# Non-local attention on one core: image 0's z in three parts, image 1's phi/g split between two places, image 1's later jobs moved by half a step

## The chip, the cores and the metric

The kernel runs on one core of a Trainium2 chip. The metric is the device time of one execution in microseconds (us), as the median of several runs. The engines that matter are TensorE (PE; its weight loads are listed as PEld), VectorE (DVE), ScalarE (ACT), GpSimd (POOL) and SyncE (SP), whose queue issues most of the DMAs.

## The reference

For each of four images x of 128 channels by 1024 pixels (32 x 32), two layers follow one another:

```python
# layer 0: no softmax, so it is one matrix per image
theta, phi, g = (W_i @ x + b_i for each)            # 64 x 1024 each
pairwise = theta.T @ phi / 1024
y = pairwise @ g.T                                   # 1024 x 64
z = x + out_w @ y.T + out_b                          # 128 x 1024
# layer 1: softmax attention on z
scores = (Wt @ z + bt).T @ (Wp @ z + bp) / sqrt(128) # 1024 x 1024
out = z + Wc @ (softmax(scores, rows) @ z.T).T + bc
```

## The kernel before, in words

Layer 0 is folded into z = A x + d with a 128 x 128 matrix A per image. The jobs for it are: `pg0` and `pg1` (phi and g of the two halves of the pixels, 4 chunks of 128 each, `phi_g_chunks`, L227, copied with the bias by DVE, `copy_pg`, L639), `MT` (their product, L245), `R` (L249), `A` (L254), `Z0` and `Z1` (L264). Layer 1 is folded into t = U z + u (jobs `t0`, `t1`, L272) and scores = t.T z, and the values V = Wc z (jobs `V0` to `V2`, L286). Each job is a group of matmuls into the one PSUM bank `aux`; an engine copies it out and only then may the next job write the bank. `AUX_ORDER` (L54) lists the jobs in their order, and the waits count along it (`aux_before`, `aux_after`). Most products are made of three matmuls of a high and a low part (`three`, L220), so each result is copied twice: ACT writes the high part, DVE or POOL what is left of it.

The attention works through 32 tiles of 128 rows (`n`, 8 per image; `t` is the tile within the image). Per tile: `scores(n)` on PE (6 matmuls of 512 columns into `ring`, two tiles deep), `row_max(n)` on DVE (L680), `row_shift(n)` on POOL (L821), `exps(n)` on ACT (L523), `norm(n)` on DVE (L688), `turn(n)` on PE (8 transposes into `turned`), `high_turned` on ACT (L531), `low_turned` on DVE (L695), and a quarter of `attend` of the group of four tiles before (6 matmuls into `numer`, from n = 4 on).

Every engine runs its own list of instructions strictly in order. The lists are written out by hand as loops over n. On PE (L438) step n is: `scores(n+2)`, the next image's `early_job(t)`, `turn(n)`, `attend`, the next image's `late_job(t)`. On ACT (L611): `late_job(t-1)`, `early_job(t)`, `high_turned(n)`, `exps(n+2)`. On DVE: `late_job(t-1)`, `row_max(n+2)`, `norm(n+1)`, `early_job(t)`, `low_turned(n)`. On POOL: `row_shift(n+2)`, then splits of x, z or the first values. The jobs of image 1 run beside the tiles of image 0, when there is nothing to attend to yet for n = 0 to 3: MT early at t = 1, R late at t = 1, A early at 2, Z0 late at 2, Z1 early at 3, t0 early at 4.

Ahead of the loop stands a prologue for image 0 with banks and semaphores of its own. Its z is made in two halves into `ring` (L385), high parts at L554, low parts at L718. Its t is made in three parts (`FIRST_T`: 128, 384 and 512 columns; L559, L725). Between these PE makes pg0 of image 1 into `aux` and pg1 into `numer`. On POOL the prologue is: the parts of U, X_hi of image 1 (L788), image 0's z as a sum of its parts (L808, twice), the first half of X_lo of image 1 (L792), `row_shift(0)`, the second half of X_lo, the split of the first values (L844, L846), `row_shift(1)`.

Of the kernel before, what the change touches and what calls it, by code (L numbers as in the profile page):

```python
# [5 lines left out]
F32 = mybir.dt.float32  # L6
# [7 lines left out]
C = 128  # L14
# [34 lines left out]

Z_BUFFERS = 3  # L50
# [4 lines left out]
AUX_ORDER = ([(0, "MT"), (0, "R"), (0, "A"), (1, "pg0"), (0, "t1")] + [(1, job) for job in JOBS[2:]]  # L55
# [19 lines left out]
def build(nc, x, pg_weights, pg_bias, inner, weights, out):  # L75
    with ExitStack() as ctx:
# [61 lines left out]
        tp_ready, tp_copied = sem("tp_ready"), sem("tp_copied")  # L138
        u_ready, u_copied, u_hi, u_lo = sem("u_ready"), sem("u_copied"), sem("u_hi"), sem("u_lo")
# [34 lines left out]

        def chunks_of(bank, part):
            first, last = V_PARTS[part]
            return bank[:, 0:(last - first) * V_COLS].rearrange("p (j c) -> p j c", c=V_COLS)


        @block.sync  # L180
        def _(sp):
            for half in range(HALVES):
                sp.dma_start(X[:, 0, columns(half)], x[0, :, columns(half)]).then_inc(first_loaded[half], 16)
            sp.dma_start(w[:, :], weights[:, 0:2 * C]).then_inc(w_loaded, 16)
            sp.dma_start(VW[:, 0:C], weights[:, W_C:W_C + C]).then_inc(conv_loaded, 16)
            sp.dma_start(X[:, 1, :], x[1]).then_inc(x_loaded[1], 16)

            def load(b):
                if b == 2:
                    sp.wait_ge(first_z, HALVES)  # L190
                else:
                    sp.wait_ge(first_pg_copied, HALVES + 1)
                    sp.wait_ge(aux_free, aux_after(1, "pg0"))
# [25 lines left out]
        def _(pe):  # L219
# [7 lines left out]
            def phi_g_chunks(b, bank, half):  # L227
                for n, j in enumerate(half_range(half)):
# [67 lines left out]
            def scores(n):  # L296
                b, t = divmod(n, TILES)
                if b == 0:
                    pe.wait_ge(first_t_lo, 1 if t == 0 else 2)
                if t == GT or (b and t == 0):  # L300
                    pe.wait_ge(aux_free, aux_after(b, "t0" if t < GT else "t1"))
                if b and t == 0:
                    pe.wait_ge(z_lo, b * HALVES)
                if n >= 2:
                    pe.wait_ge(probs_ready, n - 1)
                for half in range(HALVES):
                    if n == 0:
                        pe.wait_ge(first_z_lo, half + 1)
                    mm = scores_half(n, half)
                mm.then_inc(scores_ready, 1)  # L310
# [53 lines left out]

            pe.wait_ge(pad_ready, 2)
# [6 lines left out]
            nc.tensor.transpose(turned[:, C:2 * C], w[:, W_P:W_P + C], identity[:, :]).then_inc(tp_ready, 1)  # L372
            job_A(0)
            pe.wait_ge(tp_copied, 1)
            pe.wait_ge(bias_loaded, 16)
            theta_b, phi_b = bias[:, B_T:B_T + 1], bias[:, B_P:B_P + 1]
            UT_bank = turned[:, BANK:BANK + C + 3]
            nc.tensor.matmul(UT_bank[:, 0:C], T_w, P_w, start=True, stop=True)
            nc.tensor.matmul(UT_bank[:, C:C + 1], P_w, theta_b, start=True, stop=True)
            nc.tensor.matmul(UT_bank[:, C + 1:C + 2], T_w, phi_b, start=True, stop=True)  # L380
            nc.tensor.matmul(UT_bank[:, C + 2:C + 3], theta_b.broadcast_to([C, C]), phi_b,
                             start=True, stop=True).then_inc(u_ready, 1)
            pe.wait_ge(first_a, 1)
            for half in range(HALVES):
                nc.tensor.matmul(ring[:, 1, columns(half)], AT[:, :], X[:, 0, columns(half)],  # L385
                                 start=True, stop=True).then_inc(first_z, 1)
# [21 lines left out]
            def early_job(b, t):  # L408
                if t == 0 and b > 1:
                    job_pg(b, 0)  # L410
                if t == 1:
                    job_MT(b)
                if t == 2:
                    job_A(b)
                if t == 3:
                    job_Z(b, 1)
                if t == 4:
                    job_t(b, 0)
                if t == 5:
                    job_V(b, 1)  # L420
                if t == 6:
                    job_t(b, 1)

            def late_job(b, t):
                if t == 1 and b == 1:
                    first_value_part(2)
                if t == 0 and b > 1:
                    job_pg(b, 1)
                if t == 1:
                    job_R(b)  # L430
                if t == 2:
                    job_Z(b, 0)
# [40 lines left out]
        def _(act):  # L473
# [78 lines left out]
            for half in range(HALVES):  # L552
                act.wait_ge(first_z, half + 1)
                nc.scalar.activation(Z_hi[:, 0, columns(half)], ring[:, 1, columns(half)], ACT.Identity,  # L554
                                     bias=d[:, :]).then_inc(first_z_hi, 1)

# [20 lines left out]
            first_t_high(0)  # L577
            first_t_high(1)
# [6 lines left out]
            def early_job(b, t):  # L585
                if t == 1:
                    copy_MT(b)
                if t == 2:
                    high_A(b)
                if t == 3:  # L590
                    make_Z(b, 1)
# [7 lines left out]
            def late_job(b, t):  # L599
                if t == 1:  # L600
                    copy_R(b)
                if t == 1 and b == 1:
                    first_values(2)
                if t == 2:
                    make_Z(b, 0)
# [26 lines left out]
        def _(dve):  # L632
# [80 lines left out]
            dve.wait_ge(u_ready, 1)  # L713
            nc.vector.tensor_scalar(U[:, :], turned[:, BANK:BANK + C + 3], SCALE, None, ALU.mult).then_inc(u_copied, 1)

            def first_z_low(half):
                dve.wait_ge(first_z_hi, half + 1)
                nc.vector.scalar_tensor_tensor(out=Z_lo[:, 0, columns(half)], in0=ring[:, 1, columns(half)],  # L718
                                               scalar=d[:, :], in1=Z_hi[:, 0, columns(half)].bitcast(F32),
# [9 lines left out]
            first_z_low(0)  # L729
            first_z_low(1)  # L730
            first_t_low(0)

            make_pg(1, 0)
            dve.wait_ge(first_pg, HALVES + 1)
            copy_pg(numer[:, :], 1, first_pg_copied)
            row_max(0)
            first_t_low(1)
            norm(0)
            row_max(1)

            def early_job(b, t):
                if t == 0 and b > 1:
                    make_pg(b, 0)
                if t == 2:
                    low_A(b)
# [7 lines left out]
            def late_job(b, t):  # L753
                if t == 0 and b > 1:
                    make_pg(b, 1)
                if t == 4:
# [26 lines left out]
        def _(pool):  # L783
# [16 lines left out]
            pool.wait_ge(u_copied, 1)  # L800
            nc.gpsimd.tensor_copy(VW[:, C:C + 1], U[:, C + 1:C + 2]).then_inc(vw_ready, 1)
            nc.gpsimd.tensor_copy(UT_hi[:, :], U[:, 0:C]).then_inc(u_hi, 1)
            pool.wait_ge(u_hi, 1)
            nc.gpsimd.tensor_tensor(UT_lo[:, :], U[:, 0:C], UT_hi[:, :].bitcast(F32), ALU.subtract).then_inc(u_lo, 1)
            high_x(1)
            for half in range(HALVES):
                pool.wait_ge(first_z_lo, half + 1)
# [45 lines left out]
            for n in range(ALL - 1):  # L853
# [5 lines left out]
                if i + 1 < IMAGES:  # L859
# [7 lines left out]
                    if t == (3 if i else 2):  # L867
                        split_z(i + 1, 0)
                    if t == (4 if i else 3):
# [36 lines left out]
```

## Time and profile before

| | |
|---|---|
| time, median of 3 runs | 170.57 us (170.32 to 170.78) |
| the profiled execution | 170.84 us, span 169.0 us |
| PE busy | 161.8 us (96%) |
| DVE, ACT, POOL busy | 124.1, 95.8, 69.1 us |
| weights loads of PE (PEld) | 135.2 us, beside the matmuls |
| DMA | 4.76 MB, mean 28 GB/s |

The span is the time from the first to the last instruction in the profile, and the execution takes 1.8 us more than that. Busy shares are averages over stages with different limits: the prologue (to about 25 us), tiles 1 to 3 of image 0 (to about 42 us), the long middle, and the last tiles (from about 155 us). Starts in the trace are microseconds from the span's start. The ends of matmuls are modelled and overlap the next matmul, so the time that a group takes on PE is best read from its start to the start of what follows.

### The profile page before, as it was taken

The page shows a single profiled execution, that of the slowest core. Times are in us where ns is not written, and L with a number is a line of the kernel's source. Part 1 is how long each engine was busy: PE and PEld are TensorE (multiplying, and loading weights), DVE is VectorE, ACT ScalarE, POOL GpSimd, SP SyncE. Part 2 cuts the span into 40 slices and gives each one's busy share as a digit, 9 for nine tenths or more (in the row PEclk, how much of TensorE's full clock was granted, in tenths as well). Part 3 has the DMA queues.
Part 4 walks back from the last instruction along what each step waited for, and adds up shares of the span by engine and source line. Part 5 has one row for each costly group of instructions (what it writes and reads, how often), then busy time and mean ns, then how long its engine had stood idle before and what let it go on. Part 6 is the DMA issues. An engine that isn't in the chain of part 4 may idle for free.

```text
span 169.0 us, 2605 instructions
## 1 busy us (share of the span) xinstructions
PE 161.8 (96%) x967; PEld 135.2 (80%) x967; DVE 124.1 (73%) x211; ACT 95.8 (57%) x181; POOL 69.1 (41%) x79
## 2 busy tenths in 40 slices
PE   7889899799999999999999999999999999998994
PEld 7777778687888887887888888887888888886893
DVE  1316599869888876867888987667888898888412
ACT  3024558769557546567557656467566766576410
POOL 1009765277102295236415296216525253825030
PEclk9999999999999999999999999999999999999999
DMA  4603030000000010000001010000000110000111
GB/s 134 207 0 128 0 124 0 0 0 2 6 0 0 4 62 0 0 0 4 0 0 47 17 66 0 0 0 4 0 2 0 63 49 17 0 0 0 62 63 65
DMA packets 2829, 4.76 MB, mean 28 GB/s; under 512 B 448, under 2 KB 1280, under 8 KB 2816
## 3 DMA queue, kind: packets, MB, share of 16 engines
q1 hardware_dynamic: 2304, 4.39, 7.5%
q10 hardware_dynamic: 512, 0.20, 0.5%
q8 instruction: 8, 0.13, 0.3%
q14 instruction: 5, 0.04, 0.1%
HBM read 2.49 MB, written 2.10 MB: 27 GB/s over the span
## 4 chain that ended last, share of the span: by engine, by line
PE 84%; DVE 7%; DMA 3%; ACT 2%; POOL 2%; issue 1%; SPq 0%; ACTq 0%
PE numer L338 22%; PE turned L318 14%; PE ring L223 9%; PE ring L225 8%; PE ring L224 8%; PE aux L282 4%; DMA X<-x_dram 3%; DVE negmax L680 3%; PE aux L229 3%; PE aux L345 2%; PE aux L235 2%; PE aux L223 2%; DVE P L688 2%; ACT P L523 1%; PE aux L225 1%; PE aux L224 1%
## 5 line engine op out<-in xcount | busy, mean ns | idle before, releaser
L821 POOL TENSOR_SCALAR shift<-negmax,rho 128x1 f32<-128x1 f32 x32 | 27.6, 863 | 72.8 <-DVE negmax L680 69.8
L680 DVE TENSOR_REDUCE negmax<-ring 128x1 f32<-128x1024 f32 x32 | 39.1, 1223 | 19.0 <-PE ring L225 18.8
L523 ACT ACTIVATE P<-ring,shift 128x1024 f32<-128x1024 f32 x32 | 35.8, 1119 | 9.9 <-POOL shift L821 9.8
L695 DVE TENSOR_TENSOR PT_lo<-turned,PT_hi 128x512 fp32r<-128x512 f32 x62 | 39.7, 681 | 0.4 <-ACT PT_hi L531 0.4
L531 ACT ACTIVATE PT_hi<-turned 128x512 fp32r<-128x512 f32 x62 | 33.6, 595 | 9.4 <-PE turned L318 9.3
L318 PE MATMUL turned<-identity,P 128*128 128x128 f32 x256 | 33.6, 274 | 0.6 <-DVE PT_lo L695 0.6
L318 PEld LDWEIGHTS turned<-identity,P 128*128 128x128 f32 x256 | 29.5, 141 | 3.9 <-DVE P L688 1.0
L223 PE MATMUL ring<-Z_hi,t_hi 128*128 128x512 f32 x64 | 26.5, 414 | 0.9 <-DVE t_lo L725 0.7
L225 PE MATMUL ring<-Z_lo,t_hi 128*128 128x512 f32 x64 | 25.2, 394 | 0.0
L224 PE MATMUL ring<-Z_hi,t_lo 128*128 128x512 f32 x64 | 25.2, 393 | 0.0
L688 DVE TENSOR_SCALAR P<-P,rden 128x1024 f32<-128x1024 f32 x32 | 24.1, 754 | 1.1
L338 PE MATMUL numer<-PT_hi,V_hi 128*128 128x512 f32 x56 | 24.4, 436 | 0.0
L338 PE MATMUL numer<-PT_hi,V_lo 128*128 128x512 f32 x56 | 22.1, 394 | 0.0
L338 PE MATMUL numer<-PT_lo,V_hi 128*128 128x512 f32 x56 | 22.1, 394 | 0.0
L223 PEld LDWEIGHTS ring<-Z_hi,t_hi 128*128 128x128 f32 x64 | 12.0, 188 | 4.1 <-DVE t_lo L725 1.0
L225 PEld LDWEIGHTS ring<-Z_lo,t_hi 128*128 128x128 f32 x64 | 12.0, 188 | 2.7
L224 PEld LDWEIGHTS ring<-Z_hi,t_lo 128*128 128x128 f32 x64 | 12.1, 188 | 2.2
L338 PEld LDWEIGHTS numer<-PT_hi,V_lo 128*128 128x128 f32 x56 | 10.5, 188 | 2.6
L338 PEld LDWEIGHTS numer<-PT_lo,V_hi 128*128 128x128 f32 x56 | 10.6, 190 | 1.3
L338 PEld LDWEIGHTS numer<-PT_hi,V_hi 128*128 128x128 f32 x56 | 10.6, 189 | 1.3
L837 POOL TENSOR_TENSOR result<-attended,Z 128x512 f32<-128x512 f32 x7 | 9.0, 1292 | 4.2 <-ACT attended L541 4.2
L503 ACT ACTIVATE t_hi<-aux,U 128x512 fp32r<-128x512 f32 x7 | 4.8, 688 | 8.1 <-PE aux L225 8.0
(117 smaller groups left out, 202.1 us busy)
## 6 DMA issues: line engine op xcount, KB each, us to landing
out_dram<-result SPq DMA_DIRECT2D x7, 256.0 KB, 2.0
X<-x_dram SPq DMA_DIRECT2D x3, 512.0 KB, 3.3
X<-x_dram SPq DMA_DIRECT2D x2, 256.0 KB, 4.2
out_dram<-result SPq DMA_DIRECT2D x1, 192.0 KB, 1.9
w<-weights_dram SPq DMA_DIRECT2D x1, 128.0 KB, 5.5
wi<-inner_dram ACTq DMA_DIRECT2D x1, 64.2 KB, 5.7
pg_w<-pg_weights_dram ACTq DMA_DIRECT2D x1, 64.0 KB, 3.3
pg_b<-pg_bias_dram ACTq DMA_DIRECT2D x1, 64.0 KB, 5.5
```

The lines of the kernel that those rows point to most:

```text
L223: nc.tensor.matmul(to, left_hi, right_hi[:, cols], start=first, stop=False)
L224: nc.tensor.matmul(to, left_lo, right_hi[:, cols], start=False, stop=False)
L225: return nc.tensor.matmul(to, left_hi, right_lo[:, cols], start=False, stop=last)
L318: mm = nc.tensor.transpose(turned[:, j * TILE:(j + 1) * TILE], P[:, n % P_BUFFERS, j * TILE:(j + 1) * TILE], identity[:, :])
L338: mm = nc.tensor.matmul(numer[:, :], left[:, b % 2, chunk], right[:, g, j, :], start=(j == 0 and n == 0), stop=(j == TILES - 1 and n == 2))
L523: nc.scalar.activation(P[:, n % P_BUFFERS, :], ring[:, n % 2, :], ACT.Exp, bias=shift[:, t:t + 1], accum_out=den[:, t:t + 1]).then_inc(pro ...
L531: nc.scalar.activation(PT_hi[:, group % GROUPS, half_chunks(half), k * TILE:(k + 1) * TILE], turned[:, columns(half)].rearrange("p (j r) - ...
L680: nc.vector.tensor_reduce(negmax[:, t:t + 1], ring[:, n % 2, :], AX.X, ALU.max, negate=True).then_inc(max_ready, 1)
L688: nc.vector.tensor_scalar(P[:, n % P_BUFFERS, :], P[:, n % P_BUFFERS, :], rden[:, t:t + 1], None, ALU.mult).then_inc(probs_normed, 1)
L695: nc.vector.tensor_tensor(PT_lo[:, group % GROUPS, half_chunks(half), rows], turned[:, columns(half)].rearrange("p (j r) -> p j r", j=CHUN ...
L821: nc.gpsimd.tensor_scalar(shift[:, t:t + 1], negmax[:, t:t + 1], rho[:, b % 2, t:t + 1], rho[:, b % 2, t:t + 1], ALU.subtract, ALU.add).th ...
L837: nc.gpsimd.tensor_tensor(result[:, g, :], attended[:, g, :], Z[:, b % Z_BUFFERS, columns(g)], ALU.add).then_inc(result_ready, 1)
```

## The change

Image 0's z is made in three parts (128, 384, 512 columns), with the first score half between them. The matmuls for U's vector parts get a bank and a copy of their own. Image 1's pg0 moves ahead of the transposes, in 3 + 1 chunks, into `numer`; pg1 moves from the prologue into the loop (early job of t = 1), and MT, R, A, Z0, Z1 of image 1 each go half a step later. Of the other images nothing is changed.

```diff
+FIRST_Z = (slice(0, TILE), slice(TILE, BANK), slice(BANK, PIX))
+PG_AHEAD = 3
-AUX_ORDER = ([(0, "MT"), (0, "R"), (0, "A"), (1, "pg0"), (0, "t1")] + [(1, job) for job in JOBS[2:]]
+FIRST_JOBS = ("pg1", "MT", "R", "A", "Z0", "Z1", "t0", "V0", "V1", "V2", "t1")
+AUX_ORDER = ([(0, "MT"), (0, "R"), (0, "A"), (0, "t1")] + [(1, job) for job in FIRST_JOBS]
+        def first_z_bank(part):
+            return ring[:, 0, FIRST_Z[0]] if part == 0 else ring[:, 1, FIRST_Z[part]]
 # SP: load(2) waits for first_z 3 instead of 2; load(3) for aux_after(1, "pg1") instead of "pg0"
 # PE, prologue
+            pe.wait_ge(x_loaded[1], 16)
+            phi_g_chunks(1, numer, 0, slice(0, PG_AHEAD))
             pe.wait_ge(pad_ready, 2)
             ...
             nc.tensor.transpose(turned[:, C:2 * C], w[:, W_P:W_P + C], identity[:, :]).then_inc(tp_ready, 1)
+            phi_g_chunks(1, numer, 0, slice(PG_AHEAD, CHUNKS_PER_HALF)).then_inc(first_pg, 1)
             job_A(0)
             pe.wait_ge(tp_copied, 1)
+            UT_bank, u_bank = turned[:, BANK:BANK + C], turned[:, 2 * C:2 * C + 3]
+            nc.tensor.matmul(UT_bank, T_w, P_w, start=True, stop=True).then_inc(ut_ready, 1)
+            pe.wait_ge(first_a, 1)
+            first_z_part(0)
+            first_z_part(1)
             pe.wait_ge(bias_loaded, 16)
             ... (the three one-column matmuls of u, now into u_bank, then_inc(u_ready, 1))
-            pe.wait_ge(first_a, 1)
-            for half in range(HALVES):
-                nc.tensor.matmul(ring[:, 1, columns(half)], AT[:, :], X[:, 0, columns(half)], ...)
-            job_pg(1, 0)
             pe.wait_ge(u_lo, 1)
             pe.wait_ge(first_z_lo, 1)
+            pe.wait_ge(u_copied, 1)
             queries(0, first_t_bank(0), FIRST_T[0]).then_inc(first_t, 1)
-            phi_g_chunks(1, numer, 1).then_inc(first_pg, 1)
-            scores(0)
+            first_z_part(2)
+            pe.wait_ge(first_t_lo, 1)
+            pe.wait_ge(first_z_lo, 2)
+            scores_half(0, 0)
             queries(0, first_t_bank(1), FIRST_T[1]).then_inc(first_t, 1)
+            pe.wait_ge(first_z_lo, 3)
+            scores_half(0, 1).then_inc(scores_ready, 1)
 # PE, loop, b == 1 only: early t=1 pg1 (was MT), t=2 R (was A), t=3 Z0 (was Z1);
 #                        late  t=1 MT, then first_value_part(2) (was first_value_part(2), R),
 #                        t=2 A (was Z0), t=3 Z1 (was none)
 # ACT: prologue first_z_high(0), (1), first_t_high(0), first_z_high(2), first_t_high(1);
 #      loop, b == 1: early t=2 copy_R, t=3 make_Z(0); late t=1 copy_MT, t=2 high_A, t=3 make_Z(1)
 # DVE, prologue
+            dve.wait_ge(first_pg, HALVES + 1)
+            dve.wait_ge(aux_ready, aux_after(0, "MT"))
+            copy_pg(numer[:, :], 0, first_pg_copied)
+            dve.wait_ge(ut_ready, 1)
+            nc.vector.tensor_scalar(U[:, 0:C], turned[:, BANK:BANK + C], SCALE, None, ALU.mult).then_inc(ut_copied, 1)
             first_z_low(0)
+            dve.wait_ge(u_ready, 1)
+            nc.vector.tensor_scalar(U[:, C:C + 3], turned[:, 2 * C:2 * C + 3], SCALE, ...).then_inc(u_copied, 1)
             first_z_low(1)
             first_t_low(0)
-            make_pg(1, 0)
-            copy_pg(numer[:, :], 1, first_pg_copied)
+            first_z_low(2)
+            first_t_low(1)
             row_max(0)
-            first_t_low(1)
+            row_max(1)
             norm(0)
-            row_max(1)
 # DVE, loop, b == 1: make_pg(1, 1) early at t=1; low_A late at t=2 (was early at t=2)
 # POOL: the parts of UT wait for ut_copied alone, VW's column is copied after them;
 #       Z of image 0 waits for first_z_lo 2 and 3; the splits of z of image 1 come at t=3 and 4 (were 2 and 3)
```

## Rows read from the trace of the kernel before

**Rows 1.** The page, part 1: engine, busy us, share, instructions.
```profile
PE 161.8 (96%) x967; PEld 135.2 (80%) x967; DVE 124.1 (73%) x211; ACT 95.8 (57%) x181; POOL 69.1 (41%) x79
```
**Rows 2.** Windows: stretch, length, busy us by engine, then granted PE clock, DMA.
```profile
29.70:34.60 4.90, 3.95 (x25) 3.25 (x25) 4.07 (x9) 3.98 (x9) 1.80 (x3) 1.00 0.00 0
42.20:155.00 112.80, 112.80 (x655) 94.03 (x655) 93.06 (x157) 70.04 (x130) 45.87 (x45) 1.00 0.03 13
```
**Rows 3.** Load of image 1: issue in SP's timeline; DMA issues, us to landing.
```profile
2.59 0.43 SPq L186 DMA_DIRECT2D X<-x_dram  x1
...
X<-x_dram SPq DMA_DIRECT2D x1, 512.0 KB, 6.1
```
**Rows 4.** Timeline of the prologue: start, us, engine, line, operation [idle before it].
```profile
9.58 0.40 PE L251 MATMUL aux<-wi,MT 128*64 128x128 f32 x2 [0.46 <-ACT MT L484]
11.93 1.96 PE L385 MATMUL ring<-X,AT 128*128 128x512 f32 x4
13.13 1.49 ACT L554 ACTIVATE Z_hi<-ring,d 128x512 fp32r<-128x512 f32 x2 [1.43 <-PE ring L385]
13.73 1.05 PE L229 MATMUL aux<-pg_w,X 128*128 128x128 f32 x8
14.75 0.30 PE L223 MATMUL turned<-Z_hi,UT_hi 128*128 128x128 f32 x1
15.37 0.37 ACT L559 ACTIVATE t_hi<-turned,U 128x128 fp32r<-128x128 f32 x1 [0.75 <-PE turned L225]
16.17 0.50 PE L223 MATMUL ring<-Z_hi,t_hi 128*128 128x512 f32 x1
17.88 1.22 DVE L680 TENSOR_REDUCE negmax<-ring 128x1 f32<-128x1024 f32 x1 [0.57 <-PE ring L225]
```
**Rows 5.** Timeline, tiles 0 and 1: POOL's queue and ACT's exponentials.
```profile
17.16 1.29 POOL L792 TENSOR_TENSOR X_lo<-X,X_hi 128x512 fp32r<-128x512 f32 x1
19.45 0.37 POOL L821 TENSOR_SCALAR shift<-negmax,rho 128x1 f32<-128x1 f32 x1 [1.00 <-ACT rho L565]
19.70 0.50 PE L223 MATMUL ring<-Z_hi,t_hi 128*128 128x512 f32 x1 [0.66 <-DVE t_lo L725]
19.85 1.12 ACT L523 ACTIVATE P<-ring,shift 128x1024 f32<-128x1024 f32 x1 [0.51 <-POOL shift L821]
22.48 1.01 POOL L846 TENSOR_TENSOR V_lo<-V_plain,V_hi 128x384 fp32r<-128x384 f32 x1
23.49 0.36 POOL L821 TENSOR_SCALAR shift<-negmax,rho 128x1 f32<-128x1 f32 x1
23.88 1.11 ACT L523 ACTIVATE P<-ring,shift 128x1024 f32<-128x1024 f32 x1 [1.11 <-POOL shift L821]
```
**Rows 6.** Timeline from scores(3) to scores(4).
```profile
24.61 0.74 DVE L656 SCALAR_TENSOR_TENSOR t_lo<-aux,U,t_hi 128x512 fp32r<-128x512 f32 x1
25.23 0.47 PE L223 MATMUL ring<-Z_hi,t_hi 128*128 128x512 f32 x1 [0.25 <-ACT P L523]
26.79 1.15 PE L235 MATMUL aux<-pgT 128*64 128x64 f32 x16
28.64 0.75 DVE L688 TENSOR_SCALAR P<-P,rden 128x1024 f32<-128x1024 f32 x1
29.70 0.50 PE L223 MATMUL ring<-Z_hi,t_hi 128*128 128x512 f32 x1
```
**Rows 7.** Timeline from A of image 1 to its V0.
```profile
33.45 0.28 DVE L651 TENSOR_TENSOR AT_lo<-aux,AT_hi 128x128 fp32r<-128x128 f32 x1
33.72 1.12 ACT L523 ACTIVATE P<-ring,shift 128x1024 f32<-128x1024 f32 x1 [0.19 <-POOL shift L821]
33.79 0.50 PE L223 MATMUL aux<-X_hi,AT_hi 128*128 128x512 f32 x1 [0.95 <-DVE AT_lo L651]
38.94 0.39 PE L223 MATMUL aux<-Z_hi,UT_hi 128*128 128x512 f32 x1
42.16 0.94 PE L282 MATMUL aux<-VW,Z 128*128 128x130 f32 x6
```

More of the change, by code:

```diff
@@ L138, in build @@
         tp_ready, tp_copied = sem("tp_ready"), sem("tp_copied")
+        ut_ready, ut_copied = sem("ut_ready"), sem("ut_copied")
         u_ready, u_copied, u_hi, u_lo = sem("u_ready"), sem("u_copied"), sem("u_hi"), sem("u_lo")
@@ L189, in load @@
                 if b == 2:
-                    sp.wait_ge(first_z, HALVES)
+                    sp.wait_ge(first_z, len(FIRST_Z))
                 else:
                     sp.wait_ge(first_pg_copied, HALVES + 1)
-                    sp.wait_ge(aux_free, aux_after(1, "pg0"))
+                    sp.wait_ge(aux_free, aux_after(1, "pg1"))
                     sp.wait_ge(x_lo, (b - 2) * HALVES)
@@ L225, in three, with phi_g_chunks @@
                 return nc.tensor.matmul(to, left_hi, right_lo[:, cols], start=False, stop=last)
-            def phi_g_chunks(b, bank, half):
-                for n, j in enumerate(half_range(half)):
+            def phi_g_chunks(b, bank, half, some=slice(0, CHUNKS_PER_HALF)):
+                for n, j in list(enumerate(half_range(half)))[some]:
                     mm = nc.tensor.matmul(bank[:, n * C:(n + 1) * C], X[:, b % 2, j * TILE:(j + 1) * TILE],
@@ L297, in scores @@
                 b, t = divmod(n, TILES)
-                if b == 0:
-                    pe.wait_ge(first_t_lo, 1 if t == 0 else 2)
+                if n == 1:
+                    pe.wait_ge(first_t_lo, 2)
                 if t == GT or (b and t == 0):
@@ L306, in scores @@
                 for half in range(HALVES):
-                    if n == 0:
-                        pe.wait_ge(first_z_lo, half + 1)
                     mm = scores_half(n, half)
@@ L372, in _, with first_z_part @@
             nc.tensor.transpose(turned[:, C:2 * C], w[:, W_P:W_P + C], identity[:, :]).then_inc(tp_ready, 1)
+            phi_g_chunks(1, numer, 0, slice(PG_AHEAD, CHUNKS_PER_HALF)).then_inc(first_pg, 1)
             job_A(0)
             pe.wait_ge(tp_copied, 1)
+            UT_bank, u_bank = turned[:, BANK:BANK + C], turned[:, 2 * C:2 * C + 3]
+            nc.tensor.matmul(UT_bank, T_w, P_w, start=True, stop=True).then_inc(ut_ready, 1)
+            def first_z_part(part):
+                nc.tensor.matmul(first_z_bank(part), AT[:, :], X[:, 0, FIRST_Z[part]],
+                                 start=True, stop=True).then_inc(first_z, 1)
@@ L375, in _ @@
+            pe.wait_ge(first_a, 1)
+            first_z_part(0)
+            first_z_part(1)
             pe.wait_ge(bias_loaded, 16)
             theta_b, phi_b = bias[:, B_T:B_T + 1], bias[:, B_P:B_P + 1]
[L377 to L380, printed above, removed]
@@ L381, in _ @@
-            nc.tensor.matmul(UT_bank[:, C + 2:C + 3], theta_b.broadcast_to([C, C]), phi_b,
-                             start=True, stop=True).then_inc(u_ready, 1)
-            pe.wait_ge(first_a, 1)
-            for half in range(HALVES):
-                nc.tensor.matmul(ring[:, 1, columns(half)], AT[:, :], X[:, 0, columns(half)],
-                                 start=True, stop=True).then_inc(first_z, 1)
-            job_pg(1, 0)
+            nc.tensor.matmul(u_bank[:, 0:1], P_w, theta_b, start=True, stop=True)
@@ L389, in _ @@
+            nc.tensor.matmul(u_bank[:, 1:2], T_w, phi_b, start=True, stop=True)
+            nc.tensor.matmul(u_bank[:, 2:3], theta_b.broadcast_to([C, C]), phi_b,
+                             start=True, stop=True).then_inc(u_ready, 1)
             pe.wait_ge(u_lo, 1)
             pe.wait_ge(first_z_lo, 1)
+            pe.wait_ge(u_copied, 1)
             queries(0, first_t_bank(0), FIRST_T[0]).then_inc(first_t, 1)
-            phi_g_chunks(1, numer, 1).then_inc(first_pg, 1)
-            scores(0)
+            first_z_part(2)
@@ L410, in early_job @@
                     job_pg(b, 0)
[L411 to L416, printed above, removed]
+                if b == 1:
+                    if t == 1:
+                        job_pg(b, 1)
+                    if t == 2:
+                        job_R(b)
+                    if t == 3:
+                        job_Z(b, 0)
+                else:
+                    if t == 1:
+                        job_MT(b)
+                    if t == 2:
+                        job_A(b)
+                    if t == 3:
+                        job_Z(b, 1)
                 if t == 4:
@@ L424, in late_job @@
             def late_job(b, t):
[L425 to L432, printed above, removed]
+                if b == 1:
+                    if t == 1:
+                        job_MT(b)
+                        first_value_part(2)
+                    if t == 2:
+                        job_A(b)
+                    if t == 3:
+                        job_Z(b, 1)
+                else:
+                    if t == 0:
+                        job_pg(b, 1)
+                    if t == 1:
+                        job_R(b)
+                    if t == 2:
+                        job_Z(b, 0)
                 if t == 4:
@@ L551, in _, with first_z_high @@
             act.wait_ge(aux_free, aux_after(0, "A"))
-            for half in range(HALVES):
-                act.wait_ge(first_z, half + 1)
-                nc.scalar.activation(Z_hi[:, 0, columns(half)], ring[:, 1, columns(half)], ACT.Identity,
+            def first_z_high(part):
+                act.wait_ge(first_z, part + 1)
+                nc.scalar.activation(Z_hi[:, 0, FIRST_Z[part]], first_z_bank(part), ACT.Identity,
                                      bias=d[:, :]).then_inc(first_z_hi, 1)
+            first_z_high(0)
+            first_z_high(1)
             def first_t_high(part):
@@ L577, in _ @@
             first_t_high(0)
+            first_z_high(2)
             first_t_high(1)
@@ L585, in early_job @@
             def early_job(b, t):
[L586 to L591, printed above, removed]
+                if b == 1:
+                    if t == 2:
+                        copy_R(b)
+                    if t == 3:
+                        make_Z(b, 0)
+                else:
+                    if t == 1:
+                        copy_MT(b)
+                    if t == 2:
+                        high_A(b)
+                    if t == 3:
+                        make_Z(b, 1)
                 if t == 4:
@@ L599, in late_job @@
             def late_job(b, t):
[L600 to L605, printed above, removed]
+                if b == 1:
+                    if t == 1:
+                        copy_MT(b)
+                        first_values(2)
+                    if t == 2:
+                        high_A(b)
+                    if t == 3:
+                        make_Z(b, 1)
+                else:
+                    if t == 1:
+                        copy_R(b)
+                    if t == 2:
+                        make_Z(b, 0)
                 if t == 4:
@@ L712, in _, with first_z_low @@
             nc.vector.tensor_copy(TP[:, :], turned[:, 0:2 * C]).then_inc(tp_copied, 1)
[L713 to L719, printed above, removed]
+            dve.wait_ge(first_pg, HALVES + 1)
[3 more added lines that the diff above has]
+            nc.vector.tensor_scalar(U[:, 0:C], turned[:, BANK:BANK + C], SCALE, None, ALU.mult).then_inc(ut_copied, 1)
+            def first_z_low(part):
+                dve.wait_ge(first_z_hi, part + 1)
+                nc.vector.scalar_tensor_tensor(out=Z_lo[:, 0, FIRST_Z[part]], in0=first_z_bank(part),
+                                               scalar=d[:, :], in1=Z_hi[:, 0, FIRST_Z[part]].bitcast(F32),
                                                op0=ALU.add, op1=ALU.subtract).then_inc(first_z_lo, 1)
@@ L729, in _ @@
             first_z_low(0)
+            dve.wait_ge(u_ready, 1)
+            nc.vector.tensor_scalar(U[:, C:C + 3], turned[:, 2 * C:2 * C + 3], SCALE, None,
+                                    ALU.mult).then_inc(u_copied, 1)
             first_z_low(1)
+            dve.wait_ge(u_copied, 1)
             first_t_low(0)
-            make_pg(1, 0)
-            dve.wait_ge(first_pg, HALVES + 1)
-            copy_pg(numer[:, :], 1, first_pg_copied)
+            first_z_low(2)
+            first_t_low(1)
             row_max(0)
-            first_t_low(1)
+            row_max(1)
             norm(0)
-            row_max(1)
             def early_job(b, t):
@@ L743, in early_job @@
                     make_pg(b, 0)
-                if t == 2:
+                if t == 1 and b == 1:
+                    make_pg(b, 1)
+                if t == 2 and b > 1:
                     low_A(b)
@@ L755, in late_job @@
                     make_pg(b, 1)
+                if t == 2 and b == 1:
+                    low_A(b)
                 if t == 4:
@@ L799, in _ @@
             nc.gpsimd.memset(VW[:, C + 1:C + 2], 0.0).then_inc(vw_ready, 1)
[L800 to L801 removed]
+            pool.wait_ge(ut_copied, 1)
             nc.gpsimd.tensor_copy(UT_hi[:, :], U[:, 0:C]).then_inc(u_hi, 1)
@@ L804, in _ @@
             nc.gpsimd.tensor_tensor(UT_lo[:, :], U[:, 0:C], UT_hi[:, :].bitcast(F32), ALU.subtract).then_inc(u_lo, 1)
+            pool.wait_ge(u_copied, 1)
+            nc.gpsimd.tensor_copy(VW[:, C:C + 1], U[:, C + 1:C + 2]).then_inc(vw_ready, 1)
             high_x(1)
             for half in range(HALVES):
-                pool.wait_ge(first_z_lo, half + 1)
+                pool.wait_ge(first_z_lo, half + 2)
                 nc.gpsimd.tensor_tensor(Z[:, 0, columns(half)], Z_hi[:, 0, columns(half)].bitcast(F32),
@@ L866, in _ @@
                         split_first_values(1 if n == 0 else 2)
-                    if t == (3 if i else 2):
+                    if t == (2 if i else 3):
                         split_z(i + 1, 0)
-                    if t == (4 if i else 3):
+                    if t == 4:
                         split_z(i + 1, 1)
```

## The prediction

> **What bounds the kernel now.** I read the busy shares first, then windows, then the timeline up to 42 us. The shares name PE, 96% busy [rows 1]. The windows say where that holds: from 42.20 to 155.00 PE is busy for 112.80 of 112.80 us [rows 2]. There, no other engine decides; a delay in PE's list at 42 us arrives whole at the end, and so does a gain. The change leaves PE's list from image 1's t0 on as it is, and the other images' jobs too. So the question is only when PE reaches t0 of image 1 (38.94) and V0 (42.16) [rows 7]. Ahead of that PE is not the bound everywhere: from 29.70 to 34.60 it is busy for 3.95 of 4.90 us [rows 2].
>
> The timeline shows what else bounds. The exponential of tile 1 starts at 23.88, straight behind POOL's shift(1) at 23.49, and that has no idle before it: it stood behind V_lo of the first values [rows 5]. That split needs values that ACT copies only behind the exponential of tile 0, which waits for shift(0). Second, PE idles 0.95 at 33.79 for AT_lo before Z0 [rows 7].
>
> **The change part by part.**
>
> *Four pg chunks between the first matrices.* PE idles 0.46 before R, for MT's copy, with R at 9.58 [rows 4]. Four chunks take at most 1.02 (13.73 to 14.75), some 0.9 without the wait behind them; three take 0.66 and begin at about 9.0, so R starts at 9.7, 0.12 late. The fourth, 0.22, lies in the wait for R's copy. I take +0.13 for A's end. Image 1's x is issued at 2.59 and lands 6.1 later, at 8.69 [rows 3]: 0.3 before it is wanted. If it is late, each tenth goes onto everything behind, so 0 to +0.3; I take 0, since it lies ahead by the row. DVE copies this half while PE makes U and z.
>
> *z in three parts.* A half takes 0.9 on PE (four passes from 11.93 to 13.73) [rows 4], so 128 columns take 0.23 and 384 take 0.67. AT is copied at 11.68; part 0 runs from 11.76, part 1 to 12.66, then the three u products (at most 0.26 each by the chunks' pace, I take 0.22) to 13.3. Their copy is done at 13.75: the bound is from 0.1 (almost nothing to do) to 0.37 (the 128-column ACT copy); I take 0.2. Then t's first part starts at 13.80, not 14.75 [rows 4]: 0.95 gained. From there to the first scores it is 1.42 (14.75 to 16.17), so score half 0 starts at 15.2.
>
> But z's last part now stands behind t's first part: PE 14.15 to 15.05, high part on ACT to 15.97 (0.7 of the 1.49 for two [rows 4]), low part on DVE to 16.75. Score half 1 starts at 16.8 and row_max(0) at 17.9 to 18.0, where it was 17.88 [rows 4]. The gain for tile 0 is gone. What stays is tile 1: t's middle part is done before row_max(0), so scores(1) can start at 18.4 instead of 19.70 [rows 5].
>
> *Does that lead pass on?* POOL joins image 0's second half of z only from 16.8, for 1.26 (no row shows it alone; the nearest, X_lo of the same shape, is 1.29), then does the 1.29 of X_lo [rows 5], and is free for shift(0) at 19.35 to 19.4, where it was 19.45. From shift(0) to the exponential of tile 1 POOL's and ACT's orders are unchanged: 23.88 - 19.45 = 4.43 [rows 5]. So that exponential starts at 23.8, its sum is out at 25.0, and scores(3), waiting for it, starts at 25.15 against 25.23 [rows 6]. Of 1.3 us, 0.08 remains; PE idles 1.1 before scores(3) instead of 0.25.
>
> *pg1 and MT in step 1.* Behind scores(3) PE now does pg1 (0.9) and turn(1), to 28.4. MT comes late in that step and waits for DVE's copy of pg1, which stands behind row_max(3) and norm(2). DVE's list is closed from the exponential on: in the trace P of tile 2 ends at 28.64 + 0.75 = 29.39, 4.3 behind the sum of exponential 1 (25.08); 0.2 of that was low_t(0,1), which was busy from 24.61 to 25.35 and which is done in time now [rows 6]. So P ends at 29.1, the pg copy (0.7) at 29.8: PE idles 1.4. What queues behind MT is the third part of the first values and scores(4), for which DVE's next maximum waits. MT takes 1.07, the values 0.5: scores(4) starts at 31.4, not 29.70 [rows 6]. Late by 1.7, although R (0.37) is not yet done; it comes behind.
>
> *A and Z0.* scores(4), R, turn(2) and A take 1.49 + 0.37 + 0.87 + 0.58 = 3.3, scores(5) 1.4 more, to 36.1. Before, Z0 waited for A's low part too, but the high part was taken from A before the exponential of tile 4. Now it is the late job of t = 2, which ACT does behind that exponential. That one started 4.02 after scores(4) (33.72 - 29.70) [rows 6, 7]; so at 35.4, with its sum at 36.6, the high part at 36.8, AT_lo 0.35 later, Z0 at 37.25 (the trace has 0.34 from AT_lo's start to Z0's [rows 7]). PE idles 1.15, where it idled 0.95.
>
> *Z1 and t0.* Z0 0.8, turn(3) 0.8, Z1 behind Z0's copy (0.15 idle), then scores(6) to 41.2. t0 of image 1 needs Z1's copy, now a late job of t = 3 that ACT does behind the exponential of tile 5, at 40.0 to 41.2, so it ends at 41.8. t0 starts at 41.8 instead of 38.94: 2.9 late. Before, V0 was held 0.25 behind attend; that wait goes. V0 is 2.6 late.
>
> As a ledger from scores(3) to t0: before 13.71 (38.94 - 25.23), of which 0.95 idle; after 13.71 - 0.95 + 0.9 (pg1) + 1.4 + 1.15 + 0.15 + 0.6 of idle = 16.96, which from 25.15 ends at 42.1. Step by step I had 41.8; the 0.3 is rounding and gaps between groups, and goes into the range.
>
> A rule weighed against this: the row has the granted clock at 1.00, the 2.4 GHz level, through the stretch with the 0.95 idle [rows 2]. The Trainium skill, "TensorE: Matmul & The Clock Gate", section "A second HAM failure mode: psum-queue depth-cycling", says that short idles between groups of matmuls, when frequent, can make the clock alternate between its levels. By that rule the four idles from 24 to 42 would cost more than their length; the sum goes by the row.
>
> **Sum.** PE is 2.6 late at 42 us, all of it passes to the end: 170.84 + 2.6 = 173.4 for the profiled execution, which lay 0.27 above the median; so 173.2. The terms' bounds: shift(0) from -0.3 to +0.3, landing of x 0 to +0.3, each of the three waits +-0.3: 172.3 to 174.1.
>
> **Rivals.**
>
> *A. Only one of the two waits forms (14%).* Either the pg copy holds MT, and the copies behind the exponentials find room, or the reverse. For it: ACT had idle in 29.70 to 34.60 (3.98 of 4.90 busy) [rows 2]; against it: the order is fixed and the exponential itself comes late. Price: 2.6 less 1.15 to 1.7, so +0.9 to +1.5: 171.5 to 172.1.
>
> *B. Faster: the lead of tile 1 passes through POOL's queue (9%).* The place is shift(1). If the split of the first values didn't hold it, it would follow row_max(1), which ends at 21.1 after scores(1) from 18.4: the exponential of tile 1 would start at 21.5, 2.3 ahead of my figure. scores(3) and DVE's pg copy would both move by that, so MT's idle stays; but the exponentials of tiles 4 and 5, behind which A's and Z1's copies stand, need not then come late, and with those idles (1.15, 0.15, 0.6) gone V0 is 2.6 - 2.3 - 1.9 = 1.6 early: 169.0. It decides where lead and vanished idles together pass 2.6; the lead alone doesn't reach that. For it: scores(1) does start 1.3 earlier. Against it: shift(1) had no idle before it [rows 5].
>
> *C. No change (6%).* The lead is lost as forecast, but pg1, R and Z0 only change places and the waits are covered: the ledger is then the old 13.71 with 0.9 (pg1) for the 0.95 of idle: 170.2 to 171.0.
>
> *D. The clock falls in the idles (3%).* The matmuls between 29.8 and 41.8, some 9 us of work, would run at half the speed for part of that: +2 to +5 on top, 175 to 178. The skill's page named above has the rule; the trace has 1.00 throughout [rows 2].
>
> **Chances.** Forecast 68%, A 14%, B 9%, C 6%, D 3%. What a measurement of this kernel can tell from no change is about 0.3% (0.5 us). Faster 0.09, within 0.06, slower 0.85. The range of 171.2 to 174.2 leaves out B, most of C, D and a little of the forecast; the forecast's own range is 172.3 to 174.1.
>
> **What would show it.** The first t matmul near 13.8 and scores(1) near 18.4 show the gain in the prologue; shift(0) near 19.4 and the exponential of tile 1 near 23.8 show it lost. MT of image 1 near 29.8, released by DVE's pg copy, with PE idle ahead; Z0 near 37.2, released by AT_lo; t0 near 41.8; busy PE from V0 to 155. I am wrong if MT starts with no wait, if the exponential of tile 1 comes before 23, or if image 1's x lands after 9.

## The result and the profile after

| | before | after |
|---|---|---|
| median | 170.45 us (170.32 to 170.78, 4 runs) | 172.88 us (172.75 to 173.31, 4 runs) |
| ratio | | 1.0142, 95% interval 1.0111 to 1.0173 |
| span profiled | 169.0 us | 170.9 us |

The change made the kernel 1.4% slower. The busy shares of the page, after:

```profile
PE 161.5 (94%) x969; PEld 134.6 (79%) x969; DVE 124.7 (73%) x213; ACT 96.2 (56%) x182; POOL 69.1 (40%) x79
```

PE does as much work as before [rows 1] and idles more. Windows of after (stretch, length, busy by engine, granted clock) say where:

```profile
25.20:31.40 6.20, 4.87 (x43) 4.28 (x43) 5.59 (x9) 4.77 (x11) 2.42 (x3) 1.00 0.10 22
31.40:41.00 9.60, 8.87 (x49) 6.63 (x47) 6.84 (x12) 6.22 (x14) 4.69 (x6) 1.00 0.12 43
44.60:157.00 112.40, 112.40 (x656) 93.92 (x654) 92.57 (x156) 70.09 (x130) 46.76 (x46) 1.00 0.03 13
```

From V0 on PE is full again, as in [rows 2]. The timeline of after (start, us, engine, line, operation), prologue:

```profile
13.66 0.30 PE L232 MATMUL turned<-Z_hi,UT_hi 128*128 128x128 f32 x1 [0.34 <-DVE U L785]
17.82 1.22 DVE L730 TENSOR_REDUCE negmax<-ring 128x1 f32<-128x1024 f32 x1
18.04 0.48 PE L232 MATMUL ring<-Z_hi,t_hi 128*128 128x512 f32 x1
19.23 0.37 POOL L881 TENSOR_SCALAR shift<-negmax,rho 128x1 f32<-128x1 f32 x1
19.71 1.22 DVE L730 TENSOR_REDUCE negmax<-ring 128x1 f32<-128x1024 f32 x1 [0.67 <-PE ring L234]
22.27 1.00 POOL L906 TENSOR_TENSOR V_lo<-V_plain,V_hi 128x384 fp32r<-128x384 f32 x1
23.26 0.36 POOL L881 TENSOR_SCALAR shift<-negmax,rho 128x1 f32<-128x1 f32 x1
23.66 1.11 ACT L555 ACTIVATE P<-ring,shift 128x1024 f32<-128x1024 f32 x1 [1.85 <-POOL shift L881]
24.91 0.51 PE L232 MATMUL ring<-Z_hi,t_hi 128*128 128x512 f32 x1 [0.81 <-ACT P L555]
```

Image 0's t starts 1.1 earlier than in [rows 4] and scores(1) 1.7 earlier than in [rows 5]. row_max(1) is over by 20.93, but shift(1) starts at 23.26, straight behind V_lo. Of all the lead 0.3 is left at scores(3) [rows 6], and the second half of image 0's x landed 0.34 earlier in this execution (its phi/g start at 6.16, not 6.50, in the two timelines). So nothing of the lead is left.

The chunks of pg0 between the first matrices cost more than they seem to. First the second product of image 0's MT before, then that product, the three chunks and R after:

```profile
8.44 0.68 PE L235 MATMUL aux<-pgT 128*64 128x64 f32 x8 [0.17 <-DVE pgT L640]
8.10 0.68 PE L244 MATMUL aux<-pgT 128*64 128x64 f32 x8 [0.17 <-DVE pgT L690]
8.70 0.94 PE L238 MATMUL numer<-pg_w,X 128*128 128x128 f32 x6
9.57 0.43 PE L260 MATMUL aux<-wi,MT 128*64 128x128 f32 x2
```

From that product to R it is 1.47 now and was 1.14 (9.58 - 8.44, [rows 4]). R stands where it stood only because x landed earlier.

Then the three waits of the loop, after:

```profile
28.28 0.75 DVE L738 TENSOR_SCALAR P<-P,rden 128x1024 f32<-128x1024 f32 x1
28.95 0.68 DVE L690 TENSOR_TENSOR pgT<-aux,pg_b 128x512 f32<-128x512 f32 x1
29.68 1.15 PE L244 MATMUL aux<-pgT 128*64 128x64 f32 x16 [1.33 <-DVE pgT L690]
31.23 0.48 PE L232 MATMUL ring<-Z_hi,t_hi 128*128 128x512 f32 x1
35.22 1.12 ACT L555 ACTIVATE P<-ring,shift 128x1024 f32<-128x1024 f32 x1 [0.29 <-POOL shift L881]
36.33 0.27 ACT L524 ACTIVATE AT_hi<-aux 128x128 fp32r<-128x128 f32 x1
37.04 0.50 PE L232 MATMUL aux<-X_hi,AT_hi 128*128 128x512 f32 x1 [0.73 <-DVE AT_lo L701]
41.43 0.50 PE L232 MATMUL aux<-Z_hi,UT_hi 128*128 128x512 f32 x1 [0.27 <-ACT Z L530]
44.51 0.83 PE L291 MATMUL aux<-VW,Z 128*128 128x130 f32 x6
```

V0 is 2.35 late [rows 7]. With the earlier landing taken out it is 2.35 + 0.34 = 2.69; the forecast had 2.6. That a landing arrives whole at V0 is seen in experiment 9, whose list is that of the kernel before up to there: the product that starts at 8.44 above starts at 7.98 in its trace, and V0 at 41.70 instead of 42.16, both 0.46 earlier. So a position in a single trace is compared below only with its landing taken out; the times are medians and need no such correction.

One thing is wrong in the description of the change and in the prediction: the other images are not untouched. GpSimd's line now reads `if t == (2 if i else 3): split_z(i + 1, 0)`, so the first half of z of images 2 and 3 is split at t = 2, where it was 3. PE gives back 0.41 between V0 and the turn at 155.75 (157.69 after), the first one in the last tiles with a wait ahead of it (113.59 before, 113.18 after; 42.16 to 155.75 and 44.51 to 157.69). Experiment 9 is on that. So the spans differ by 2.69 - 0.34 - 0.41 = 1.9.

### The profile page after: what moved, and what is told of

The parts are those of the page before. It is cut to its first block, busy times and chain, and to the rows that moved or that the text cites. A ratio compares the mean times of both kernels' runs of the same rounds, so it can differ in the third digit from the quotient of the medians.

```text
span 170.9 us, 2607 instructions
## 1 busy us (share of the span) xinstructions
PE 161.5 (94%) x969; PEld 134.6 (79%) x969; DVE 124.7 (73%) x213; ACT 96.2 (56%) x182; POOL 69.1 (40%) x79
## 4 chain that ended last, share of the span: by engine, by line
PE 79%; DVE 6%; ACT 5%; POOL 4%; DMA 3%; issue 1%; SPq 0%; ACTq 0%
PE numer L345 22%; PE turned L325 14%; PE ring L232 7%; PE ring L234 7%; PE ring L233 7%; PE aux L291 4%; DMA X<-x_dram 3%; ACT P L555 3%; PE aux L352 2%; PE aux L244 2%; DVE negmax L730 2%; PE aux L238 2%; PE aux L232 2%; PE aux L234 2%; PE aux L233 1%; DVE P L738 1%
```

## Experiments

All edits are to the changed kernel, unless it says otherwise. Times are medians, ratios are to the kernel before on the same chip.

**1. The loop alone (loop_only).** The prologue of before, with only pg1 taken out, and the changed loop.

```diff
-            phi_g_chunks(1, numer, 1).then_inc(first_pg, 1)   # prologue of before
+                    if t == 1: job_pg(b, 1)                    # and the changed loop, on PE, ACT, DVE
+                    if t == 3: split_z(i + 1, 0)               # POOL, every image
```

> The prologue of the kernel before with the changed kernel's loop for image 1 (pg1 in step 1, MT, R, A, Z0, Z1 half a step later, z's splits on POOL at t = 3 and 4 for every image). Theory (the loop's waits are the whole loss): scores(3) at 25.2 as before, MT waits for the pg copy and starts near 29.8, t0 near 41.7, V0 near 44.7; V0 is 2.5 late and the time is 172.7 to 173.2. Rival (the loss lies in the prologue, the chunks and parts put there): V0 near 42.2, 170.3 to 170.9.

173.05 us, ratio 1.0154 (1.0135 to 1.0174). MT at 29.80 behind 1.40 idle, t0 at 41.52, V0 at 44.59: 2.43 late, 2.60 with a landing 0.17 earlier than before taken out, and 2.60 in time. The loop alone is the whole loss; it is a little more than that of the change because the z of images 2 and 3 is split no earlier here.

**2. The prologue alone (prologue_only).** The loop of before; pg1 behind the first values.

```diff
             value_chunks(0, numer, 0).then_inc(first_v, 1)
+            job_pg(1, 1)
@@ DVE
             row_max(0)
+            make_pg(1, 1)
             row_max(1)
```

> The changed kernel's prologue with the loop of the kernel before; pg1 of image 1 is put behind the first values on TensorE and between the two first maxima on VectorE. Theory (the prologue's lead is eaten by GpSimd's queue, and costs nothing else): scores(1) near 19.0, exponential of tile 1 near 23.7 as in the changed kernel, scores(3) near 24.9, V0 of image 1 0.3 earlier than before (41.9); 170.0 to 170.5. Rival (the prologue loses): 171.5 or more. Rival (the lead passes on): 169.3 or less.

170.55 us, 1.0006 (0.9996 to 1.0015): no change, 0.05 over the theory's range and far from both rivals. scores(1) at 18.77, the exponential of tile 1 at 23.54, V0 at 41.78. V0's 0.38 is no gain: R at 9.40 shows a landing 0.17 earlier than in the changed kernel's trace, so 0.51 earlier than before. The new prologue neither wins nor loses with GpSimd's queue as it is. That queue costs it twice: V_lo holds shift(1), and norm(0), which starts at 21.77 beside V_lo, takes 1.50 instead of 0.75.

**3. The pg copy first (pg_copy_first).**

```diff
+                if n == 1: make_pg(1, 1)
                 if n + 2 < ALL:
                     row_max(n + 2)
```

> The changed kernel, with VectorE's copy of pg1 ahead of row_max(3) instead of behind norm(2). Theory (MT waits for that copy): the copy is done near 28.2, MT starts right behind turn(1) near 28.3 instead of 29.68, scores(4) and all behind it are 1.3 earlier; 171.4 to 171.8. Rival (the 0.9 us of pg1 on TensorE and the later copies decide, the wait is cover for them): 172.6 to 172.9.

171.57 us, 1.0066 (1.0050 to 1.0082). MT starts at 28.26 right behind turn(1), scores(4) at 29.80, V0 at 43.12: 1.4 of PE, 1.3 of time. The rival falls.

**4. The copies ahead (copies_ahead).**

```diff
+                if n == 2: high_A(1)
+                if n == 3: make_Z(1, 1)
                 if n + 2 < ALL:
                     exps(n + 2)       # ACT; both are gone from late_job
```

> The changed kernel, with ScalarE's high part of A ahead of the exponential of tile 4 and its copy of Z1 ahead of that of tile 5, instead of behind them. Theory (these two copies stood behind the exponentials): Z0 near 36.5 instead of 37.04 (VectorE is busy with PT_lo until 36.1), t0 with no idle behind scores(6), so V0 0.7 to 0.9 earlier; 172.0 to 172.3. Rival (something else holds Z0 and t0, such as GpSimd's split of z, which ends at 41.07): under 0.3 gained, 172.6 to 172.9.

172.04 us, 1.0099 (1.0084 to 1.0115). Z0 at 36.41, t0 at 40.59 with no idle, V0 at 43.63, 0.88 earlier, of which 0.09 is the landing (R at 9.48, not 9.57). In time it is 0.84.

**5. GpSimd's queue in another order (pool_order).**

```diff
-            low_x(1, 0)
             row_shift(0)
-            low_x(1, 1)
-            split_first_values(0)
             row_shift(1)
+            split_first_values(0)
@@ loop, behind row_shift(n + 2)
+                    if n in (0, 1): low_x(1, n)
```

> The changed kernel, with GpSimd's queue in another order: both halves of X_lo of image 1 and the split of the first values go behind shift(0) and shift(1) (values directly behind shift(1), the X_lo halves behind shift(2) and shift(3)). Theory (the lead of tile 1 was held in that queue): the exponential of tile 1 starts near 21.9 instead of 23.66 and scores(3) near 23.1 instead of 24.91; from there VectorE's list (two maxima, two norms, PT_lo, t_lo) is the next bound, so its pg copy starts near 28.2 instead of 28.95 and only 0.7 of 1.8 reaches V0: 172.0 to 172.3. Rival (the lead was not held by GpSimd): scores(3) stays at 24.9, 172.7 to 173.0. Rival (the whole lead arrives): 171.0 to 171.3.

175.16 us, 1.0273 (1.0242 to 1.0304): outside all the ranges given. The part that was tested holds: the exponential of tile 1 starts at 21.82. But then, in the timeline:

```profile
24.07 1.30 POOL L851 TENSOR_TENSOR X_lo<-X,X_hi 128x512 fp32r<-128x512 f32 x1
24.40 1.52 DVE L738 TENSOR_SCALAR P<-P,rden 128x1024 f32<-128x1024 f32 x1
29.76 1.97 PE L244 MATMUL aux<-pgT 128*64 128x64 f32 x16 [1.93 <-DVE pgT L690]
```

The exponential is 1.84 earlier than in the changed kernel, norm(1) only 0.69 (24.40, not 25.09), since row_max(2) and the low part of t stand ahead of it in DVE's list. And norm(1) takes 1.52, not 0.75, beside GpSimd's X_lo. So the pg copy is no earlier than in the changed kernel (29.02, not 28.95), while PE, now early, waits 1.93 for it. Windows of the same kernel:

```profile
26.00:28.00 2.00, 1.35 (x10) 0.84 (x9) 2.00 (x3) 0.67 (x2) 1.28 (x2) 1.00 0.00 0
28.00:29.70 1.70, 0.00 (x0) 0.00 (x0) 1.66 (x5) 0.79 (x2) 1.28 (x2) 0.89 0.00 0
31.70:35.30 3.60, 3.60 (x11) 2.65 (x10) 0.00 (x0) 0.75 (x3) 0.00 (x0) 0.50 0.41 141
35.30:37.00 1.70, 1.70 (x12) 1.29 (x12) 1.48 (x3) 0.52 (x2) 0.18 (x1) 0.75 0.00 0
37.00:38.00 1.00, 1.00 (x10) 0.96 (x9) 1.00 (x2) 1.00 (x3) 1.00 (x2) 1.00 0.00 0
```

The means of the second and the fourth window, 0.89 and 0.75, put the fall at about 29.3, 1.5 us into the wait, and the rise at about 36.15. Between them the granted clock is 0.50, the 1.2 GHz level. MT takes 1.97 instead of 1.15. This is rival D of the prediction.

**6. The same with the wait filled (pool_order_warm).**

```diff
+                        pe.wait_ge(first_v_copied, 2)
+                        keep_warm(numer[:, 0:C], 32)
                         job_MT(b)
```

> The pool_order kernel with 32 idle bf16 matmuls of 128 columns (1.8 us of work at full clock) in TensorE's wait for the pg copy, into the free bank numer, ahead of MT; they compute nothing that is used. Theory (the 3 us that pool_order lost came from the granted clock, which fell to 0.5 behind that wait): the clock stays at 1.00 from 20 to 45, MT near 29.7 lasts 1.15 and not 1.97, V0 near 44.4; 172.3 to 172.9. Rival (the new order itself delays work by GpSimd's later X_lo): over 174.

173.14 us, 1.0151 (1.0137 to 1.0165), 0.25 over the range I gave. The clock is 1.00 in every window from 20 to 42, MT takes 1.15, V0 is at 44.95. So the clock cost 2.0 us of time in experiment 5, and with the clock kept that kernel is still no better than the changed one (172.88): norm(1), at 1.51 again, eats the lead.

**7. All three repairs (all_three)**, the edits of experiments 3, 4 and 5 together.

> The changed kernel with the three repairs together: pg copy ahead of row_max(3), A's and Z1's copies ahead of the exponentials, GpSimd's queue in the new order. Theory (the three waits are what ate the change's gain, and they add): MT near 27.0, scores(4) near 28.6, V0 near 41.0 instead of 44.51; 169.2 to 169.9, faster than the kernel before. Rival (they hide one another; VectorE is then the bound in tiles 1 to 4): V0 near 42, 170.3 to 170.9.

170.69 us, 1.0007 (0.9995 to 1.0020). MT at 27.67, V0 at 42.15 (R at 9.30 shows that 0.27 of it is an earlier landing than in the changed kernel's trace): a smaller gain than the theory's, and the rival's number. norm(1) takes 1.51 here too. t0 waits another 0.48 for GpSimd's Z_lo, which is the next thing late.

**8. GpSimd's order on the kernel before (before_pool), and on the kernel of experiment 2 (pro_pool).**

> The kernel before, with GpSimd's queue alone in the new order. Theory (without the changed prologue the order matters little, since row_max(1) ended at 23.17 and shift(1) started at 23.49): scores(3) 0.3 earlier, 170.0 to 170.4. Rival (GpSimd's queue was the bound of the prologue by itself): 169.5 or less.

171.07 us, 1.0034 (1.0020 to 1.0048): slower, and outside both ranges given.

> The changed kernel's prologue and the loop of the kernel before (the prologue_only kernel), with GpSimd's queue in the new order. Theory (prologue's lead is real once that queue lets it pass, and the old loop has no wait of the new one): exponential of tile 1 near 22.4, scores(3) near 23.7, V0 of image 1 near 41.2 (VectorE bound between); 169.6 to 170.1, faster than before by 0.4 to 0.8. Rival (VectorE and GpSimd collide more, nothing gained): 170.3 or more.

170.60 us, 1.0009 (0.9990 to 1.0027): no gain, the rival's number. In both the X_lo half stands behind shift(2), at 25.11 and 24.74, where norm(1) is due, and norm(1) takes 1.88. In pro_pool:

```profile
24.70 1.88 DVE L711 TENSOR_SCALAR P<-P,rden 128x1024 f32<-128x1024 f32 x1
24.74 1.29 POOL L821 TENSOR_TENSOR X_lo<-X,X_hi 128x512 fp32r<-128x512 f32 x1
```

The order that releases shift(1) puts GpSimd's two-input work beside DVE's norm.

**9. The earlier split of z alone (before_z_split)**, on the kernel before.

```diff
-                    if t == (3 if i else 2):
+                    if t == 2:
                         split_z(i + 1, 0)
```

> The kernel before, with one change: GpSimd splits the first half of z of images 2 and 3 at t = 2 instead of 3, as the changed kernel does. Theory (this is what gave back 0.3 us between V0 of image 1 and the end): t0 of images 2 and 3 starts without its wait, 0.17 earlier each, V0 of image 1 unchanged at 42.16; 0.3 less, 170.0 to 170.3. Rival (the give-back came of something else): no change, 170.4 to 170.6.

170.19 us, 0.9984 (0.9973 to 0.9996). From V0 of image 1 to t0 of image 2 it is 35.38 where it was 35.54, and to the first turn with a wait 113.39 where it was 113.59. That is 0.20 of the 0.41. Another 0.11 is V0 itself, 0.83 in the changed kernel and 0.94 in [rows 7]: the kernel of experiment 1 has the short V0 and not the earlier split, and takes 113.51 over the same stretch, 0.08 less. For the last 0.1 the runs show no cause.

**10. All three, with the X_lo halves left in their place (three_split_late).** In the order of experiment 5 only the split of the first values moves.

```diff
             row_shift(0)
             low_x(1, 1)
-            split_first_values(0)
             row_shift(1)
+            split_first_values(0)
```

> The all_three kernel, but GpSimd's X_lo halves stay where the changed kernel has them; only the split of the first values goes behind shift(1). Theory (GpSimd's two-input X_lo at 24.0 doubled VectorE's norm(1) from 0.75 to 1.51, and that held all behind it): norm(1) takes 0.75, MT near 27.0 instead of 27.67, V0 near 41.4 instead of 42.15; 169.7 to 170.2, faster than the kernel before by 0.3 to 0.8. Rival (VectorE's list is not what bounds here): V0 near 42.1, 170.5 to 170.8.

169.96 us, 0.9963 (0.9950 to 0.9976). norm(1) takes 0.75, MT starts at 27.22, V0 at 41.70. It is 0.73 of time under experiment 7, and the only edit between the two is where 2.6 us of GpSimd's work stand.

**11. The best of it: the new prologue, the old loop with pg1 as in experiment 2, the late split of values, the early split of z (pro_split_late).**

> The changed kernel's prologue, the old loop, pg1 in the prologue; on GpSimd only the split of the first values goes behind shift(1), and the first half of z of images 2 and 3 is split one step earlier, as in the changed kernel. Theory: scores(3) near 23.9 or later by its place behind turn(0), norm(1) at 0.75, V0 near 41.4, 0.3 more given back later by the z splits; 169.5 to 170.1. Rival (the lead is lost between VectorE and ScalarE in tiles 2 to 4 again): V0 at 41.8 or later, 170.2 to 170.6.

169.51 us, 0.9945 (0.9932 to 0.9957), faster than both kernels. In its timeline:

```profile
21.81 0.91 POOL L851 TENSOR_SCALAR shift<-negmax,rho 128x1 f32<-128x1 f32 x1 [1.10 <-DVE negmax L703]
21.82 0.75 DVE L711 TENSOR_SCALAR P<-P,rden 128x1024 f32<-128x1024 f32 x1
24.55 0.75 DVE L711 TENSOR_SCALAR P<-P,rden 128x1024 f32<-128x1024 f32 x1
25.70 1.15 PE L244 MATMUL aux<-pgT 128*64 128x64 f32 x16
41.09 0.94 PE L291 MATMUL aux<-VW,Z 128*128 128x130 f32 x6
```

shift(1) follows its maximum, norm(0) and norm(1) are short, and MT has no wait. V0 is 1.07 earlier than in [rows 7], of which 0.47 is the landing (image 0's second MT product at 7.97, not 8.44): 0.60 by the kernel. The time is 0.93 less; the earlier split of z alone gave 0.25 (experiment 9).

The late split was not run with the old prologue. But in the kernel before, shift(1) starts at 23.49 and row_max(1), from 21.95 for 1.22, ends at 23.17, so the move could bring at most 0.3 at that place. With the new prologue, shift(1) is 1.2 earlier than before with the landing taken out (21.81 + 0.47 against 23.49).

## Why the prediction was right, point by point

- *PE bounds from 42 us on, so a delay there passes to the end.* Right: 112.40 of 112.40 from V0 on. It passed less 0.41, half of which I missed because I did not see the change to the other images' split.
- *The chunks between the first matrices cost nearly nothing.* Under-priced: forecast +0.12 at R and +0.13 at A's end, measured +0.33 at R (1.47 for 1.14) and +0.36 at A's copy (from the second MT product to it 3.19, 11.29 - 8.10, where it was 2.83, 11.27 - 8.44). The three chunks take 0.87 to R's start, not 0.66. R's own number, 9.57 against a forecast of 9.7, is close by luck: the landing was 0.34 early. Image 1's x did land in time, though barely: in experiment 7, where image 0's landing is 0.36 earlier still, the chunks start at 8.43 released by that DMA.
- *z in three parts brings t forward.* Forecast 13.80, measured 13.66: the landing was 0.34 early, and the chunks cost 0.23 more than forecast. row_max(0) forecast 17.9 to 18.0, measured 17.82. scores(1) forecast 18.4, measured 18.04; from t to there it took 4.38, where the forecast had 4.6.
- *GpSimd's queue holds the lead.* Right: shift(0) at 19.23 (19.35 to 19.4), from it to the exponential of tile 1 4.43 as before, the exponential at 23.66 (23.8), scores(3) at 24.91 (25.15). Of the 0.08 that was to remain nothing does: scores(3) is 0.32 early, the landing 0.34. Experiment 5 moved the exponential to 21.82 by that queue alone.
- *MT waits for the pg copy.* Forecast at 29.8 with 1.4 idle, measured 29.68 with 1.33. Experiment 3 gives it back: 1.3 us.
- *A's and Z1's copies stand behind the exponentials.* Z0 forecast 37.25, measured 37.04; t0 41.8 and 41.43. Both idles were smaller than forecast (0.73 of 1.15; 0.27 of 0.6), while the groups between took longer: scores(4) to scores(5) 3.44 (31.23 to 34.67), where the forecast had 3.3. Experiment 4 gives 0.8 back.
- *The wait before V0 goes.* Forecast 0.25, measured 0.14: from t0 to V0 it is 3.08 (41.43 to 44.51) and was 3.22 (38.94 to 42.16).
- *The total.* Forecast +2.6, measured +2.43 by the medians (170.45 and 172.88). That these agree is in part luck: V0 was 0.1 later than forecast, and the give-back was not foreseen.
- *Rivals A and C, one wait or none.* Both waits formed, and experiments 3 and 4 took each away by itself, for 1.3 and 0.8 us.
- *Rival B, the lead passes.* Its condition was named rightly, shift(1), but its price was too high. It had the lead reach the exponentials of tiles 4 and 5 and end A's and Z1's waits; in experiment 6, with shift(1) released and the clock kept, the lead was gone by the pg copy, and Z0 still waited 0.73 and t0 0.30. And I took no price for what GpSimd's work does to DVE; experiments 5 to 8 paid it. With the work kept apart, experiment 11 got 0.9 us, 0.25 of it by the split of z.
- *Rival D, the clock.* Not in this change: 1.00 in every window, with idles of 0.8, 1.3, 0.7. One step further, at 1.93 idle in a stretch that had 1.35 of 2.00 busy ahead, it fell. In the changed kernel the same stretch, 26 to 28, was busy for 2.00 of 2.00, so the runs don't tell the length of the idle from what came before it. "TensorE: Matmul & The Clock Gate" of the Trainium skill, section "A second HAM failure mode: psum-queue depth-cycling", has frequent short idles between groups of matmuls as a cause of an alternating clock. The trace of experiment 5 shows one fall behind one wait, and no alternation, so it neither bears the sentence out nor speaks against it.

## What to carry to other kernels

Moving a job by half a step moves its copies in the queues of three other engines; for each, read what stands ahead of it there, since that (here an exponential or a norm) decides and not the matmul. A lead won on one engine is worth nothing until the in-order queue that releases the next stage is followed: here the new prologue was worth nothing (experiment 2) until one split moved behind shift(1) (experiment 11). When a repair shortens work ahead of a wait, look at the granted clock too: the wait gets longer, and the clock can fall.

## What the runs showed of the hardware

- DVE's norm and GpSimd's work do not run side by side at full speed. Alone, norm takes 0.75 and X_lo 1.28 to 1.30. Together X_lo keeps its time and the norm takes 1.51 to 1.88; each time the norm ends 0.54 to 0.55 after GpSimd's instruction does. That holds for all eight norms so met in the first 50 us of six traces: beside X_lo (experiments 5 to 8), V_lo (experiment 2, 1.50) and Z_lo (both kernels of experiment 8, 1.09 and 1.11). Beside the one-column shift it is the other way round: shift takes about 0.9 instead of 0.37, and the norm keeps its 0.75 (0.91 and 0.75 in the timeline of experiment 11).
- The order of the starts in the trace does not tell which of the two pays when they are close. norm(1) starts 0.04 ahead of X_lo in pro_pool and pays; shift starts 0.01 ahead of norm(0) in experiment 11 and pays.
- DVE's row_max, which reads PSUM, is not slowed by X_lo: 1.22 at 17.82 in the changed kernel, with X_lo from 17.92 to 19.20.
- The granted clock fell from 1.00 to 0.50 some 1.5 us into an idle of 1.93 us on TensorE, and stayed there for 6.8 us, although TensorE was busy without a gap from 29.76 on, 6.4 of them. 32 idle matmuls in the wait kept it at 1.00 and saved 2.0 us.
